# The first convolution layer of a graph network with its two products in the other order

## The chip, the cores and the metric

The kernel runs on one core of one Trainium2 chip. The core has five engines that run their own instruction streams and wait for each other by semaphores: TensorE (PE, matrix products into PSUM), VectorE (DVE), ScalarE (ACT), GpSimd (POOL) and SyncE (SP, which here only starts transfers). A transfer is carried out by 16 DMA engines. The metric is the device time of one execution in microseconds; the median of some executions is compared.

## The reference

`x` has 128 samples of 128 nodes with 128 features. A layer of graph convolution multiplies by weights, adds a bias, multiplies by the adjacency matrix over the nodes and cuts below zero. Two such layers, then four passes of an LSTM over windows of 1, 2, 3 and 4 nodes, a residual sum with a normalization, then a graph attention with another residual sum and normalization.

```
h = relu(einsum('ts,bsh->bth', adj, x @ Wg0 + bg0))
h = relu(einsum('ts,bsh->bth', adj, h @ Wg1 + bg1))
for p in range(1, 5):
    wins = h[:, :nw * p, :].reshape(Bv * nw, p, Hd)
    last = _lstm_last(Wih[p-1], Whh[p-1], bih[p-1], bhh[p-1], wins)
    h = h.at[:, idx, :].set(last.reshape(Bv, nw, Hd))
x = layernorm(x + h)
x = layernorm(x + attention(x, W_lin, W_val, a, W_out, adj, src, dst))
```

## The kernel before

Everything is computed to about single precision. Some products are plain FP32 products: a 128x128 by 128x128 product then appears as two records ("passes") in the trace. Others are made of three F32R products over 512 columns: each operand is split into a rounded part (`_hi`) and the rest (`_lo`), and hi*hi, lo*hi and hi*lo are added in PSUM.

**Stages.** The span has three parts. The first (to about 211 us) is the convolution stage, fused with the LSTM pass over windows of one node. The second is the LSTM passes over 2, 3 and 4 nodes (lines 429 to 474 on TensorE). The third is the attention (function `back`). This case is about the first.

**Slots.** The samples are cut into 32 tiles of four samples, 512 columns each. The first stage runs through 38 slots. It is a pipeline written out by hand: slot n works on tile n in the first product, tile n-1 in the second, and so on. Each engine has its own `slot(n)` function that gives its order of work, and runs it strictly in that order. On TensorE slot n does:

- L361: x times adjacency (bank AX), tile n, four FP32 products with the x tile of one sample stationary
- L351 to L353: the LSTM's input gate, tile n-5, three F32R products
- L379: times Wg0 (bank H1), tile n-1, four FP32 products
- L351 to L353: the candidate gate G, tile n-5
- L389: times adjacency (bank AH), tile n-2, four FP32 products
- L351 to L353: the output gate, tile n-5
- L402 to L406: bias and times Wg1 (bank H2), tile n-3, four F32R products

On ScalarE: L510 relu and rounding of bank H2 into hT_hi, L515 copy of bank AX into axT, L500 for gates I and G, L524 rounding of bank AH, L529 tanh of the cell, L500 for the output gate. On VectorE: L709 output (gate times tanh), L713 rest of H2 into hT_lo (semaphore h2_done), L719 and L721 split of the output, L730 relu of bank H1 into h1, L737 cell value (semaphore c_ready, which L529 waits for), L741 rest of bank AH.

**What else lies between slots.** After some slots TensorE turns a piece of LSTM weights (L285, four transposes), ScalarE rounds it (L492, w_hi) and VectorE takes the rest (L700, w_lo). `piece_slot` puts these after slots 2, 11, 14, 17, 20, 23 and 26. The text calls it a cut. After slots 0 to 6 come small preparations for the attention: `rank_rows` after slot 0 and `sort_edges` after slot 1 (L314, L317) on TensorE. On VectorE `degrees`, `rank_edges` and `rank_rows` (lines 578 to 630, up to L603) stand ahead of slot 0, since they only prepare tables; L586 in `degrees` sums the LSTM biases once they are loaded. L634 reads what sort_edges has made.

**Transfers.** SyncE loads x tiles into a ring of three (L232), each as soon as L361 has read the tile three before it. The tile has nodes on partitions, and the four samples' rows of 128 features are 512 bytes each. Wg0 is requested right behind the first tile. ScalarE's queue loads biases and Wg1 at the start. For the third stage a second array, x_by_feature, with features first, is loaded.

Of the kernel before, what the change touches and what calls it, by code (L numbers as in the profile page):

```python
# [7 lines left out]
F32 = mybir.dt.float32  # L8
F32R = mybir.dt.float32r
# [3 lines left out]
P = 128  # L13
# [9 lines left out]
BT = 4  # L23
# [62 lines left out]
        self.bias = sb("bias", [P, SKIPS * GATES])  # L86


def front(nc, sb, sem, tables, hT_hi, hT_lo, ident, adj_sb, psum, x, adj, Wg0, bg0, Wg1, bg1, Wih, Whh, bih, bhh,
          W_lin, W_val, a, W_out, src, dst):  # L90

    B = x.shape[0]
    tiles = B // BT
    phases = lstm_phases(B)
    TW = BT * P
    HEADS, DH = a.shape  # L100
# [19 lines left out]
    tanh_c = [work[:, 11 + s, :] for s in range(2)]  # L120
    h_full = [work[:, 13 + s, :] for s in range(2)]

    axT = [work[:, s, :] for s in range(2)]
    h1 = [work[:, 2 + s, :].rearrange("p (b h) -> p b h", b=BT) for s in range(2)]
    X_RING = 3
    x_tile = [work[:, k, :].rearrange("p (b d) -> p b d", b=BT) for k in (8, 10, 11)]
    w_raw = [work[:, k, :].rearrange("p (g d) -> p g d", g=GATES) for k in (5, 13)]

    adjT = sb("adjT", [P, P])
    wg0 = sb("wg0", [P, P])  # L130
    wg1 = sb("wg1", [P, P])
    wg1_hi = sb("wg1_hi", [P, P], F32R)
# [42 lines left out]
    names = ("ident_zero ident_ready consts zeros row_ones adj_loaded wg0_loaded wg1_loaded bg0_loaded bg1_loaded col_loaded b_loaded "  # L175
             "adjT_psum adjT_ready neg_bg0 degree_psum degree_ready by_ready ranks_psum deg_hi bias_hi deg_ready bias_ready "
             "b_summed b_psum b_ready wg1_cut wg1_ready w_psum w_hi_ready w_lo_ready "
             "ax_psum axT_ready h1_psum h1_ready ah_psum ahT_hi ahT_ready h2_psum h2_hi h2_done "
             "gates_read f_ready ig_ready tanh_ready fc_done ig_done c_ready h_mul h_hi h_done tiles_done "
             "rows_loaded cols_loaded a_loaded iota_done a_zero tables_f ecol_done key_done spreads ranks permutes rows_psum rows_ready "  # L180
             "row_edges onehots w_means w_centred wT_psum wT_ready adj_psum adj_done eps_done log_done diag_done log_psum log_ready ends_ready sames shifted caps")
# [3 lines left out]
    gate_psum = [sem(f"f_gate_psum_{n}") for n in "ifgo"]  # L185
    CREDIT = 2

    AX, H1, AH, H2 = range(4)
    GATE_BANK = {I: 4, G: 5, O: 6}
    SIDE = 7  # L190

# [4 lines left out]
    def has(k):  # L196
        return 0 <= k < tiles
# [31 lines left out]

    def run_sync(sp):  # L230
        def load_x(k):
            sp.dma_start(x_tile[k % X_RING], x[k * BT:(k + 1) * BT].rearrange("b t d -> t b d")).then_inc(x_loaded[k % X_RING], 16)  # L232

        def load_piece(i):
            p, j = pieces[i]
            s, _ = raw_of(i)
            sp.dma_start(w_raw[s], (Wih, Whh)[j][p].rearrange("(g h) d -> h g d", g=GATES)).then_inc(raw_loaded[s], 16)

        sp.dma_start(adj_sb[:, :], adj).then_inc(S["adj_loaded"], 16)
        load_x(0)  # L240
        sp.dma_start(wg0[:, :], Wg0).then_inc(S["wg0_loaded"], 16)
        sp.dma_start(edge_row_i[:, :], src.rearrange("(a e) -> a e", a=1).broadcast_to([P, E])).then_inc(S["rows_loaded"], 16)
        load_x(1)
        load_piece(0)
        for j, w in enumerate((W_lin, W_val, W_out)):
            sp.dma_start(w_raw[1][:, j, :], w).then_inc(raw_loaded[1], 16)
        load_x(2)
        for n in range(SLOTS):
            if has(n) and has(n + X_RING):
                sp.wait_ge(S["ax_psum"], n + 1)  # L250
                load_x(n + X_RING)
            if n == piece_slot[0]:
                sp.wait_ge(S["w_psum"], 1)
                load_piece(1)
                sp.wait_ge(S["wT_psum"], 1)
                load_piece(2)
            elif n in piece_slot and piece_slot.index(n) + 2 < len(pieces):
                i = piece_slot.index(n)
                sp.wait_ge(S["w_psum"], i + 1)
                load_piece(i + 2)  # L260
# [16 lines left out]
    def run_tensor(pe, entry):  # L277
# [77 lines left out]
        def slot(n):  # L355
            if has(n):
                pe.wait_ge(x_loaded[n % X_RING], 16 * (n // X_RING + 1))
                if n:
                    pe.wait_ge(S["axT_ready"], n)
                for b in range(BT):  # L360
                    mm = pe.matmul(psum[:, AX, b * P:(b + 1) * P], x_tile[n % X_RING][:, b, :], adjT[:, :], start=True, stop=True)  # L361
                mm.then_inc(S["ax_psum"], 1)
            if has(n - 5):
                if n == 5:
                    pe.wait_ge(S["w_lo_ready"], 1)
                    pe.wait_ge(S["b_ready"], 1)
                    pe.wait_ge(S["deg_ready"], 1)
                    pe.wait_ge(S["bias_ready"], 1)
                    pe.wait_ge(S["rows_ready"], 2)
                gate_product(I, n - 5)  # L370
            if has(n - 1):
                k = n - 1
                pe.wait_ge(S["axT_ready"], k + 1)
                if k:
                    pe.wait_ge(S["h1_ready"], k)
                else:
                    pe.wait_ge(S["wg0_loaded"], 16)
                for b in range(BT):
                    mm = pe.matmul(psum[:, H1, b * P:(b + 1) * P], axT[k % 2][:, b * P:(b + 1) * P], wg0[:, :], start=True, stop=True)  # L379
                mm.then_inc(S["h1_psum"], 1)  # L380
            if has(n - 5):
                gate_product(G, n - 5)
            if has(n - 2):
                k = n - 2
                pe.wait_ge(S["h1_ready"], k + 1)
                if k:
                    pe.wait_ge(S["ahT_ready"], k)
                for b in range(BT):
                    mm = pe.matmul(by_batch(psum[:, AH, :])[:, b, :], h1[k % 2][:, b, :], adjT[:, :], start=True, stop=True)  # L389
                mm.then_inc(S["ah_psum"], 1)  # L390
            if has(n - 5):
                gate_product(O, n - 5)
            if has(n - 3):
                k = n - 3
                if k:
                    pe.wait_ge(S["h2_done"], k)
                else:
                    pe.wait_ge(S["deg_ready"], 1)
                    pe.wait_ge(S["bias_ready"], 1)
                    pe.wait_ge(S["wg1_ready"], 1)  # L400
                out, cols = psum[:, H2, :], block_of(k)
                pe.matmul(out, bias_rows[:, :], deg_rows[:, :, :], start=True, stop=False)  # L402
                pe.wait_ge(S["ahT_ready"], k + 1)
                pe.matmul(out, wg1_hi[:, :], hT_hi[:, cols], start=False, stop=False)
                pe.matmul(out, wg1_hi[:, :], hT_lo[:, cols], start=False, stop=False)
                pe.matmul(out, wg1_lo[:, :], hT_hi[:, cols], start=False, stop=True).then_inc(S["h2_psum"], 1)  # L406
# [69 lines left out]
    def run_scalar(act, entry):  # L476
# [29 lines left out]
        def slot(n):  # L506
            if has(n - 4):
                k = n - 4
                act.wait_ge(S["h2_psum"], k + 1)
                act.activation(hT_hi[:, block_of(k)], psum[:, H2, :], ACT.Relu).then_inc(S["h2_hi"], 1)  # L510
            if has(n):
                act.wait_ge(S["ax_psum"], n + 1)
                if n >= 2:
                    act.wait_ge(S["h1_psum"], n - 1)
                act.activation(axT[n % 2], psum[:, AX, :], ACT.Copy).then_inc(S["axT_ready"], 1)  # L515
            if has(n - 5):
                if n == 5:
                    act.wait_ge(S["b_ready"], 1)
                gate_of(I, n - 5)
                gate_of(G, n - 5)  # L520
            if has(n - 2):
                k = n - 2
                act.wait_ge(S["ah_psum"], k + 1)
                act.activation(hT_hi[:, block_of(k)], psum[:, AH, :], ACT.Copy).then_inc(S["ahT_hi"], 1)  # L524
            if has(n - 5):
                k = n - 5
                act.wait_ge(S["c_ready"], k + 1)
                act.wait_ge(S["h_mul"], CREDIT + k)
                act.activation(tanh_c[1], cell[1], ACT.Tanh).then_inc(S["tanh_ready"], 1)  # L529
                gate_of(O, k)  # L530
# [46 lines left out]
    def run_vector(dve, entry):  # L577
# [125 lines left out]
        def slot(n):  # L703
# [12 lines left out]
            if has(n - 6):  # L716
# [3 lines left out]
                dve.wait_ge(S["h_hi"], k + 1)  # L720
                dve.tensor_tensor(hT_lo[:, block_of(k)], h_full[1], hT_hi[:, block_of(k)].bitcast(F32),  # L721
                                  ALU.subtract).then_inc(S["tiles_done"], 1)
            if has(n - 1):
                k = n - 1
                dve.wait_ge(S["h1_psum"], k + 1)
# [24 lines left out]
        dve.tensor_scalar(bg0_all[:, :], bg0_all[:, :], -1.0, None, ALU.mult).then_inc(S["neg_bg0"], 1)  # L750
        dve.wait_ge(S["adjT_psum"], 1)
        dve.tensor_copy(adjT[:, :], psum[:, SIDE, 0:P]).then_inc(S["adjT_ready"], 1)
        degrees()
        rank_edges()
        rank_rows()
# [660 lines left out]
    return Part(S, 0, None, run_sync, run_gpsimd, run_tensor, run_scalar, run_vector), entry  # L1416


def program(nc, x, xt, adj, Wg0, bg0, Wg1, bg1, Wih, Whh, bih, bhh, W_lin, W_val, a, W_out, src, dst, out):
    B = x.shape[0]  # L1420
    with ExitStack() as ctx:
        def held(name, shape, dt=F32):
            return ctx.enter_context(nc.sbuf_tensor(name, shape, dt))
# [10 lines left out]

        with ExitStack() as room:
            first = front(nc, lambda name, shape, dt=F32: room.enter_context(nc.sbuf_tensor(name, shape, dt)), sem, tables, hT_hi, hT_lo,
                          ident, adj_sb, psum, x, adj, Wg0, bg0, Wg1, bg1, Wih, Whh, bih, bhh, W_lin, W_val, a, W_out, src, dst)
        with ExitStack() as room:
            second, entry = back(nc, lambda name, shape, dt=F32: room.enter_context(nc.sbuf_tensor(name, shape, dt)), sem, tables, first,
                          hT_hi, hT_lo, ident, psum, xt, a, src, out)  # L1440
# [52 lines left out]
```

## Time and profile before

| | |
|---|---|
| median of 3 runs | 916.77 us |
| the three runs | 914.58, 916.77, 917.51 us |
| profiled execution, its own time | 916.78 us |
| its span | 915.0 us |
| busy TensorE, VectorE, ScalarE, GpSimd | 96%, 76%, 67%, 19% |
| convolution stage with the first LSTM pass | to about 211 us |

The span runs from the first to the last instruction of the profile; the rest of the execution's time lies around it. An engine counts as busy while it executes an instruction, also when several overlap in its pipeline. On TensorE a record's duration includes the drain of the array, so the next record starts before it ends, and what a product costs is the time from its start to the next start. "Idle before" names the time that an engine stood still ahead of an instruction and which instruction or transfer released it.

### The profile page before, as it was taken

What the parts mean: (1) busy time and instruction counts of PE and PEld (TensorE: products, weight loads), DVE (VectorE), ACT (ScalarE), POOL (GpSimd) and SP (SyncE); (2) the same over time, 40 slices, a digit from 0 to 9 for tenths busy, and PEclk for the clock granted to TensorE, in tenths of its full rate; (3) what the DMA queues carried; (4) which work ended last, traced back from release to release, by engine and by line L of the source; (5) the groups of instructions that cost most, each with busy time, mean ns of one, the idle gap of its engine ahead of it and who ended that gap; (6) DMA issues with size and microseconds to landing.
All of it is one profiled execution on the core that took longest, in us unless ns stands there. A gap on an engine that the chain in (4) does not pass through costs nothing.

```text
span 915.0 us, 15431 instructions
## 1 busy us (share of the span) xinstructions
PE 876.2 (96%) x5411; PEld 761.5 (83%) x5411; DVE 694.7 (76%) x1560; ACT 612.2 (67%) x1116; POOL 175.0 (19%) x509
## 2 busy tenths in 40 slices
PE   6999999999999999999999999999998999999795
PEld 6888888877787779999998887877787888887684
DVE  4777777777778787778777777676787887886885
ACT  1777777777777666676676666666786677775344
POOL 0000000000000000000000010012564455655665
PEclk9999999999999999999999999999999999999998
DMA  4211221001000000000000177775360011111122
GB/s 108 73 47 58 70 59 47 24 1 47 1 1 0 1 1 1 1 1 1 1 1 1 29 156 162 161 183 139 81 151 1 25 36 31 29 37 47 36 70 70
DMA packets 43260, 45.44 MB, mean 50 GB/s; under 512 B 2576, under 2 KB 40112, under 8 KB 40112
## 3 DMA queue, kind: packets, MB, share of 16 engines
q1 hardware_dynamic: 39504, 27.47, 10.5%
q0 software_dynamic: 2304, 16.78, 9.0%
q8 instruction: 44, 0.72, 0.3%
q10 hardware_dynamic: 1376, 0.22, 0.1%
q14 instruction: 32, 0.26, 0.1%
HBM read 19.29 MB, written 8.39 MB: 30 GB/s over the span
## 4 chain that ended last, share of the span: by engine, by line
PE 76%; DVE 8%; DMA 6%; issue 5%; ACT 2%; POOL 1%; ACTq 0%; DVEq 0%; POOLq 0%
PE psum L443 7%; PE psum L444 7%; PE psum L445 7%; PE psum L1135 6%; PE psum L1062 6%; PE psum L461 5%; PE psum L457 5%; PE psum L458 5%; DMA hT_lo<-x_stage 3%; PE psum L361 3%; PE psum L379 3%; PE psum L389 3%; PE psum L1146 2%; PE psum L1118 2%; PE psum L352 2%
## 5 line engine op out<-in xcount | busy, mean ns | idle before, releaser
L561 ACT ACTIVATE work<-psum,bias 128x512 f32<-128x512 f32 (+1 forms) x408 | 233.3, 623 | 29.2 <-PE psum L461 28.6
L443 PE MATMUL psum<-hT_hi,w_hi 128*128 128x512 f32 (+1 forms) x408 | 148.7, 365 | 3.3 <-ACT work L561 2.6
L444 PE MATMUL psum<-hT_lo,w_hi 128*128 128x512 f32 (+1 forms) x408 | 147.4, 361 | 0.0
L445 PE MATMUL psum<-hT_hi,w_lo 128*128 128x512 f32 (+1 forms) x408 | 147.2, 361 | 0.0
L545 ACT ACTIVATE work<-work 128x512 f32<-128x512 f32 (+1 forms) x112 | 63.8, 570 | 104.4 <-DVE work L813 73.1
L973 POOL DMA_DIRECT2D hT_lo<-hT_hi x8 | 7.3, 918 | 558.5 <-DVE hT_lo L788 539.3
L820 DVE TENSOR_TENSOR work<-work 128x512 f32<-128x512 f32 (+1 forms) x112 | 68.5, 612 | 54.1 <-ACT work L545 54.1
L457 PE MATMUL psum<-hs_hi,w_hi 128*128 128x512 f32 (+1 forms) x288 | 103.8, 360 | 0.8 <-DVE hs_hi L786 0.7
L461 PE MATMUL psum<-hs_lo,w_hi 128*128 128x512 f32 (+1 forms) x288 | 104.4, 362 | 0.0
L458 PE MATMUL psum<-hs_hi,w_lo 128*128 128x512 f32 (+1 forms) x288 | 103.1, 358 | 0.0
L443 PEld LDWEIGHTS psum<-hT_hi,w_hi 128*128 128x128 f32 x408 | 76.8, 188 | 17.5 <-ACT work L561 5.4
L445 PEld LDWEIGHTS psum<-hT_hi,w_lo 128*128 128x128 f32 x408 | 76.8, 188 | 10.8
L444 PEld LDWEIGHTS psum<-hT_lo,w_hi 128*128 128x128 f32 x408 | 76.8, 188 | 10.0
L500 ACT ACTIVATE work<-psum,bias 128x512 f32<-128x512 f32 x96 | 64.9, 682 | 27.0 <-PE psum L353 24.6
L806 DVE TENSOR_TENSOR work<-work 128x512 f32<-128x512 f32 (+1 forms) x112 | 68.2, 609 | 19.1 <-ACT work L561 19.1
L1135 PE MATMUL psum<-from_node,va 128*128 128x128 f32 x512 | 63.7, 278 | 5.0 <-DVE x_kept L1364 4.4
L1062 PE MATMUL psum<-w_qv,y_ordered 128*128 128x128 f32 x512 | 63.7, 277 | 3.4 <-DVE hT_lo L1305 3.4
L1135 PEld LDWEIGHTS psum<-from_node,va 128*128 128x128 f32 x512 | 59.7, 192 | 7.4 <-issue 4.8
L1062 PEld LDWEIGHTS psum<-w_qv,y_ordered 128*128 128x128 f32 x512 | 60.7, 193 | 3.8 <-issue 3.6
L461 PEld LDWEIGHTS psum<-hs_lo,w_hi 128*128 128x128 f32 x288 | 54.0, 188 | 10.2 <-DVE hs_lo L788 4.0
L457 PEld LDWEIGHTS psum<-hs_hi,w_hi 128*128 128x128 f32 x288 | 54.1, 188 | 9.5 <-DVE hs_hi L786 3.0
L1012 POOL TENSOR_TENSOR rstd<-var_eps,minus_half 128x4 f32<-128x4 f32 (+1 forms) x49 | 60.5, 1235 | 3.8
(191 smaller groups left out, 1856.4 us busy)
## 6 DMA issues: line engine op xcount, KB each, us to landing
work<-x SPq DMA_DIRECT2D x32, 256.0 KB, 3.0
x_stage<-x_by_feature SPq DMA_DIRECT2D x8, 1024.0 KB, 5.2
hT_lo<-hT_hi POOLq DMA_DIRECT2D x8, 1024.0 KB, 9.2
hT_lo<-x_stage POOLq DMA_DIRECT2D x8, 1024.0 KB, 7.0
out<-x_kept SPq DMA_DIRECT2D x32, 256.0 KB, 2.3
work<-L_gnn_Wih SPq DMA_DIRECT2D x4, 256.0 KB, 3.0
work<-L_gnn_Whh SPq DMA_DIRECT2D x3, 256.0 KB, 3.0
bg_all<-L_gnn_bg ACTq DMA_DIRECT2D x2, 64.0 KB, 5.6
```

Of the source, the lines that this page charges most:

```text
L443: pe.matmul(out, w_hi[:, w, g, :], xh, start=True, stop=False)
L444: pe.matmul(out, w_hi[:, w, g, :], xl, start=False, stop=False)
L445: mm = pe.matmul(out, w_lo[:, w, g, :], xh, start=False, stop=(t == 0))
L457: pe.matmul(out, w_hi[:, w, g, :], hh, start=False, stop=False)
L458: pe.matmul(out, w_lo[:, w, g, :], hh, start=False, stop=False)
L461: pe.matmul(out, w_hi[:, w, g, :], hl, start=False, stop=True).then_inc(gate_psum[g], 1)
L500: op = act.activation(gate[1][g], psum[:, GATE_BANK[g], :], ACT.Tanh if g == G else ACT.Sigmoid, bias=bias[:, g:g + 1])
L561: op = act.activation(gate[s][g][:, 0:ph.width], psum[:, 4 * s + g, 0:ph.width], ACT.Tanh if g == G else ACT.Sigmoid, bias=bias[:, b:b + 1])
L806: op = dve.tensor_tensor(i_g, gate[s][I][:, 0:ph.width], gate[s][G][:, 0:ph.width], ALU.mult)
L820: dve.tensor_tensor(h_full[s][:, 0:ph.width], gate[s][O][:, 0:ph.width], tanh_c[s][:, 0:ph.width], ALU.mult).then_inc(S["h_mul"], 1)
L1062: mm = pe.matmul(psum[:, bank, b * P:(b + 1) * P], y_ordered[:, k % 2, b, :], w, start=True, stop=True)
L1135: mm = pe.matmul(psum[:, sum_bank(k), b * P:(b + 1) * P], va[:, k % 2, c, b * P:(b + 1) * P], from_node[:, c, :], start=(c == 0), stop=(c ...
```

## The change

The first layer, relu(adj (x Wg0 + bg0)), is computed as adj times (x Wg0) in place of (adj x) times Wg0.

- The first product of slot n (bank now called XW) multiplies the x tile by Wg0, in four FP32 products as before. Since the x tile is the stationary operand and is contracted over features, it now has to lie with features on partitions: the host gives the array x_by_batch, 32 tiles of 128 features by 512 values, and a tile is one run of 2 KB on each partition.
- ScalarE's L515 writes the rounded part xw_hi (in buffers that the LSTM uses only later) in place of axT. VectorE gets a new operation, xw_lo = bank XW - xw_hi, between L721 and L730 of a slot. It signals xw_ready.
- The second product of slot n multiplies by the adjacency as three F32R products of 512 columns with adjT_hi and adjT_lo stationary, in place of four FP32 products.
- TensorE's first product of slot n waits for xw_ready of slot n-1 (bank XW is free only then), where it waited for ScalarE's axT_ready. In slot 0 it waits for Wg0.
- adjT is split once, behind L752.

```diff
-    axT = [work[:, s, :] for s in range(2)]
+    xw_hi, xw_lo = hs_hi, hs_lo
+    adjT_hi = sb("adjT_hi", [P, P], F32R)
+    adjT_lo = sb("adjT_lo", [P, P], F32R)
 def load_x(k):
-            sp.dma_start(x_tile[k % X_RING], x[k * BT:(k + 1) * BT].rearrange("b t d -> t b d")).then_inc(x_loaded[k % X_RING], 16)
+            sp.dma_start(x_tile[k % X_RING], xb[k]).then_inc(x_loaded[k % X_RING], 16)
 TensorE, slot
             if has(n):
                 pe.wait_ge(x_loaded[n % X_RING], 16 * (n // X_RING + 1))
                 if n:
-                    pe.wait_ge(S["axT_ready"], n)
+                    pe.wait_ge(S["xw_ready"], n)
+                else:
+                    pe.wait_ge(S["wg0_loaded"], 16)
                 for b in range(BT):
-                    mm = pe.matmul(psum[:, AX, b * P:(b + 1) * P], x_tile[n % X_RING][:, b, :], adjT[:, :], start=True, stop=True)
-                mm.then_inc(S["ax_psum"], 1)
+                    mm = pe.matmul(psum[:, XW, b * P:(b + 1) * P], x_tile[n % X_RING][:, b, :], wg0[:, :], start=True, stop=True)
+                mm.then_inc(S["xw_psum"], 1)
             if has(n - 1):
                 k = n - 1
-                pe.wait_ge(S["axT_ready"], k + 1)
                 if k:
                     pe.wait_ge(S["h1_ready"], k)
                 else:
-                    pe.wait_ge(S["wg0_loaded"], 16)
-                for b in range(BT):
-                    mm = pe.matmul(psum[:, H1, b * P:(b + 1) * P], axT[k % 2][:, b * P:(b + 1) * P], wg0[:, :], start=True, stop=True)
-                mm.then_inc(S["h1_psum"], 1)
+                    pe.wait_ge(S["adjT_split"], 1)
+                pe.wait_ge(S["xw_ready"], k + 1)
+                out = psum[:, H1, :]
+                pe.matmul(out, adjT_hi[:, :], xw_hi[:, k % 2], start=True, stop=False)
+                pe.matmul(out, adjT_lo[:, :], xw_hi[:, k % 2], start=False, stop=False)
+                pe.matmul(out, adjT_hi[:, :], xw_lo[:, k % 2], start=False, stop=True).then_inc(S["h1_psum"], 1)
 ScalarE, slot
-                act.wait_ge(S["ax_psum"], n + 1)
+                act.wait_ge(S["xw_psum"], n + 1)
                 if n >= 2:
                     act.wait_ge(S["h1_psum"], n - 1)
-                act.activation(axT[n % 2], psum[:, AX, :], ACT.Copy).then_inc(S["axT_ready"], 1)
+                act.activation(xw_hi[:, n % 2], psum[:, XW, :], ACT.Copy).then_inc(S["xw_hi"], 1)
 VectorE, slot, between L721 and L730
+            if has(n):
+                dve.wait_ge(S["xw_hi"], n + 1)
+                dve.tensor_tensor(xw_lo[:, n % 2], psum[:, XW, :], xw_hi[:, n % 2].bitcast(F32), ALU.subtract).then_inc(S["xw_ready"], 1)
 VectorE, behind L752
+        dve.wait_ge(S["adjT_ready"], 1)
+        dve.tensor_copy(adjT_hi[:, :], adjT[:, :]).then_inc(S["adjT_cut"], 1)
+        dve.wait_ge(S["adjT_cut"], 1)
+        dve.tensor_tensor(adjT_lo[:, :], adjT[:, :], adjT_hi[:, :].bitcast(F32), ALU.subtract).then_inc(S["adjT_split"], 1)
```

## Rows read from the trace of the kernel before

**Rows 1.** The page: busy time, share of the span, instructions of each engine.
```profile
PE 876.2 (96%) x5411; PEld 761.5 (83%) x5411; DVE 694.7 (76%) x1560; ACT 612.2 (67%) x1116; POOL 175.0 (19%) x509
```
**Rows 2.** Timeline of TensorE, slot 17: start us, us, engine, line, operation, [idle before].
```profile
103.64 1.06 PE L379 MATMUL psum<-wg,work 128*128 128x128 f32 x8
104.45 0.48 PE L351 MATMUL psum<-hT_hi,w_hi 128*128 128x512 f32 x1
...
105.24 1.06 PE L389 MATMUL psum<-adjT,work 128*128 128x128 f32 x8
```
**Rows 3.** Timeline of TensorE, slot 33, where no L361 and no L379 is left.
```profile
194.59 0.39 PE L351 MATMUL psum<-hT_hi,w_hi 128*128 128x512 f32 x1
...
195.29 0.40 PE L351 MATMUL psum<-hT_hi,w_hi 128*128 128x512 f32 x1
```
**Rows 4.** Timeline of VectorE, slot 31 and the first operation of slot 32.
```profile
184.45 0.69 DVE L709 TENSOR_TENSOR work<-work 128x512 f32<-128x512 f32 x1 [0.53 <-ACT work L500]
...
188.16 0.69 DVE L737 TENSOR_TENSOR work<-work 128x512 f32<-128x512 f32 x1 [0.73 <-ACT work L500]
...
190.18 0.69 DVE L709 TENSOR_TENSOR work<-work 128x512 f32<-128x512 f32 x1 [0.53 <-ACT work L500]
```
**Rows 5.** Timelines of VectorE and ScalarE, the rest of slot 32.
```profile
193.05 0.68 DVE L737 TENSOR_TENSOR work<-work 128x512 f32<-128x512 f32 x1
...
195.07 0.69 DVE L709 TENSOR_TENSOR work<-work 128x512 f32<-128x512 f32 x1 [0.59 <-ACT work L500]
...
194.31 0.67 ACT L500 ACTIVATE work<-psum,bias 128x512 f32<-128x512 f32 x1
194.88 0.59 ACT L510 ACTIVATE hT_hi<-psum 128x512 fp32r<-128x512 f32 x1
```
**Rows 6.** Timelines of TensorE, ScalarE, VectorE around the cut after slot 11.
```profile
72.51 0.60 PE L285 MATMUL psum<-ident,work 128*128 128x128 f32 x4
72.94 1.06 PE L361 MATMUL psum<-adjT,work 128*128 128x128 f32 x8
...
73.14 0.60 ACT L492 ACTIVATE w_hi<-psum 128x512 fp32r<-128x512 f32 x1 [0.32 <-PE psum L285]
...
73.77 0.69 DVE L700 TENSOR_TENSOR w_lo<-psum,w_hi 128x512 fp32r<-128x512 f32 x1 [1.38 <-ACT w_hi L492]
74.38 0.68 DVE L709 TENSOR_TENSOR work<-work 128x512 f32<-128x512 f32 x1
```
**Rows 7.** Timeline of VectorE, the start.
```profile
11.87 0.28 DVE L586 TENSOR_TENSOR b_sum<-b_raw 16x128 f32<-16x128 f32 x1 [2.94 <-DMA b_raw<-L_gnn_bhh]
...
17.98 0.69 DVE L730 TENSOR_TENSOR work<-psum,neg_bias 128x512 f32<-128x512 f32 x1
19.78 0.69 DVE L634 COPY permute<-psum 128x512 f32<-128x512 f32 x1 [1.10 <-PE psum L317]
...
23.19 0.69 DVE L741 TENSOR_TENSOR hT_lo<-psum,hT_hi 128x512 fp32r<-128x512 f32 x1 [0.62 <-ACT hT_hi L524]
```
**Rows 8.** Timeline of TensorE, the start, slots 0, 1, 4 and 5.
```profile
7.03 2.07 PE L361 MATMUL psum<-adjT,work 128*128 128x128 f32 x8 [1.33 <-DMA work<-x]
...
12.99 2.08 PE L361 MATMUL psum<-adjT,work 128*128 128x128 f32 x8
...
16.57 2.39 PE L314 MATMUL psum<-permute,spread 128*128 128x256 f32 x8
...
30.89 0.49 PE L402 MATMUL psum<-deg_rows,bias_rows 66*128 66x512 f32 x1 [0.54 <-DVE hT_lo L713]
...
31.93 1.06 PE L361 MATMUL psum<-adjT,work 128*128 128x128 f32 x8
```
**Rows 9.** Windows of the start: each engine's busy time, granted clock, DMA share, GB/s.
```profile
12.00:16.00 4.00, 4.00 (x19) 3.64 (x19) 3.89 (x19) 0.60 (x1) 0.00 (x0) 1.00 0.02 4
```
**Rows 10.** DMA queues, packets, MB, share: 0 to 12 us, then 212 to 224 us.
```profile
q1 hardware_dynamic: 3470, 1.75, 60.7%
...
q1 hardware_dynamic: 144, 1.05, 25.1%
```

More of the change, by code:

```diff
@@ L86, in __init__, with front @@
         self.bias = sb("bias", [P, SKIPS * GATES])
-def front(nc, sb, sem, tables, hT_hi, hT_lo, ident, adj_sb, psum, x, adj, Wg0, bg0, Wg1, bg1, Wih, Whh, bih, bhh,
+def front(nc, sb, sem, tables, hT_hi, hT_lo, ident, adj_sb, psum, xb, adj, Wg0, bg0, Wg1, bg1, Wih, Whh, bih, bhh,
           W_lin, W_val, a, W_out, src, dst):
-    B = x.shape[0]
-    tiles = B // BT
+    tiles = xb.shape[0]
+    B = tiles * BT
     phases = lstm_phases(B)
@@ L121, in front @@
     h_full = [work[:, 13 + s, :] for s in range(2)]
-    axT = [work[:, s, :] for s in range(2)]
+    xw_hi, xw_lo = hs_hi, hs_lo
     h1 = [work[:, 2 + s, :].rearrange("p (b h) -> p b h", b=BT) for s in range(2)]
     X_RING = 3
-    x_tile = [work[:, k, :].rearrange("p (b d) -> p b d", b=BT) for k in (8, 10, 11)]
+    x_tile = [work[:, k, :].rearrange("p (b t) -> p b t", b=BT) for k in (8, 10, 11)]
     w_raw = [work[:, k, :].rearrange("p (g d) -> p g d", g=GATES) for k in (5, 13)]
     adjT = sb("adjT", [P, P])
+    adjT_hi = sb("adjT_hi", [P, P], F32R)
+    adjT_lo = sb("adjT_lo", [P, P], F32R)
     wg0 = sb("wg0", [P, P])
@@ L177, in front @@
              "b_summed b_psum b_ready wg1_cut wg1_ready w_psum w_hi_ready w_lo_ready "
-             "ax_psum axT_ready h1_psum h1_ready ah_psum ahT_hi ahT_ready h2_psum h2_hi h2_done "
+             "xw_psum xw_hi xw_ready adjT_cut adjT_split h1_psum h1_ready ah_psum ahT_hi ahT_ready h2_psum h2_hi h2_done "
              "gates_read f_ready ig_ready tanh_ready fc_done ig_done c_ready h_mul h_hi h_done tiles_done "
@@ L186, in front @@
     CREDIT = 2
-    AX, H1, AH, H2 = range(4)
+    XW, H1, AH, H2 = range(4)
     GATE_BANK = {I: 4, G: 5, O: 6}
@@ L249, in run_sync @@
             if has(n) and has(n + X_RING):
-                sp.wait_ge(S["ax_psum"], n + 1)
+                sp.wait_ge(S["xw_psum"], n + 1)
                 load_x(n + X_RING)
@@ L1416, in back, with program @@
     return Part(S, 0, None, run_sync, run_gpsimd, run_tensor, run_scalar, run_vector), entry
-def program(nc, x, xt, adj, Wg0, bg0, Wg1, bg1, Wih, Whh, bih, bhh, W_lin, W_val, a, W_out, src, dst, out):
-    B = x.shape[0]
+def program(nc, xb, xt, adj, Wg0, bg0, Wg1, bg1, Wih, Whh, bih, bhh, W_lin, W_val, a, W_out, src, dst, out):
+    B = xb.shape[0] * BT
     with ExitStack() as ctx:
@@ L1436, in program @@
             first = front(nc, lambda name, shape, dt=F32: room.enter_context(nc.sbuf_tensor(name, shape, dt)), sem, tables, hT_hi, hT_lo,
-                          ident, adj_sb, psum, x, adj, Wg0, bg0, Wg1, bg1, Wih, Whh, bih, bhh, W_lin, W_val, a, W_out, src, dst)
+                          ident, adj_sb, psum, xb, adj, Wg0, bg0, Wg1, bg1, Wih, Whh, bih, bhh, W_lin, W_val, a, W_out, src, dst)
         with ExitStack() as room:
@@ L1478 @@
     nc = bacc.Bacc("TRN2", target_bir_lowering=False, num_devices=1, dynamic_dma_scratch_size=1024)
-    arrays, args = {}, []
-    for name in _INPUTS:
-        array = np.ascontiguousarray(inputs[name])
-        arrays[name] = array
-        args.append(nc.dram_tensor(name, array.shape, mybir.dt.from_np(array.dtype), kind="ExternalInput").ap())
-    B, N, D = arrays["x"].shape
-    group = lstm_phases(B)[-1].batches
-    by_feature = arrays["x"].reshape(B // group, group // BT, BT, N, D).transpose(0, 4, 1, 3, 2)
-    arrays["x_by_feature"] = np.ascontiguousarray(by_feature).reshape(B // group, D, group * N)
-    args.insert(1, nc.dram_tensor("x_by_feature", arrays["x_by_feature"].shape, F32, kind="ExternalInput").ap())
-    args.append(nc.dram_tensor("out", arrays["x"].shape, F32, kind="ExternalOutput").ap())
+    arrays = {name: np.ascontiguousarray(inputs[name]) for name in _INPUTS}
+    x = arrays.pop("x")
+    B, N, D = x.shape
+    group = lstm_phases(B)[-1].batches
+    by_state = x.reshape(B // group, group // BT, BT, N, D).transpose(0, 4, 1, 3, 2)
+    arrays = {"x_by_batch": np.ascontiguousarray(x.reshape(B // BT, BT, N, D).transpose(0, 3, 1, 2)),
+              "x_by_state": np.ascontiguousarray(by_state).reshape(B // group, D, group * N), **arrays}
+    args = [nc.dram_tensor(name, array.shape, mybir.dt.from_np(array.dtype), kind="ExternalInput").ap() for name, array in arrays.items()]
+    args.append(nc.dram_tensor("out", x.shape, F32, kind="ExternalOutput").ap())
     program(nc, *args)
```

## The prediction

> **What bounds the kernel now.** I read first the engines' shares: TensorE is busy 96% of the span, VectorE 76%, ScalarE 67% [rows 1]. That says who leads on average; what the change is worth is read from the stage that it touches, so the next view is TensorE in order of time in one slot of the convolution stage. There every FP32 block of four products (eight passes) holds TensorE 0.81 us, 103.64 to 104.45, and a group of three F32R products of 512 columns that follows an FP32 block holds it 0.79 us, 104.45 to 105.24, with no idle time between [rows 2]. Further on, where a group of three follows F32R products, it takes 0.70 us, 194.59 to 195.29: its first record is 0.39 us long and not 0.48 [rows 3]. So the change of kind costs 0.09 us besides the products. The third view is VectorE over the same slots: a slot lasts 190.18 - 184.45 = 5.73 us, and L737 starts after 0.73 us of idle time, released by ScalarE's gate, which had waited for TensorE [rows 4]. TensorE sets the pace, with VectorE close behind.
>
> How close is to be seen one slot later, where TensorE has no L361 block to do and is the faster one. There L737 starts straight behind L730, at 193.05, with no idle time, and the next L709 comes at 195.07, after tanh and output gate on ScalarE [rows 5]. From L709 to L709 this is 195.07 - 190.18 = 4.89 us [rows 4, 5]. This is a closed loop: VectorE runs L709, L713, L719, L721, L730, L737 in order, ScalarE's L529 needs L737, the output gate L500 follows L529, the next L709 needs that gate. It goes round in 4.89 us whatever TensorE does; up to slot 31 it has 5.73 - 4.89 = 0.84 us to spare.
>
> **The change part by part.**
>
> *The second product.* Removed in each slot is L379's FP32 block, added three F32R products with adjT_hi and adjT_lo stationary. Block and G group took 0.81 + 0.79; now both follow F32R products and take 0.70 each. Saving 1.60 - 1.40 = 0.20 us a slot, so a full slot would last 5.53. There are 28 slots that have both (5 to 32): 5.6 us, if TensorE stays the bound. The first product keeps form and count (x stationary, Wg0 moving) and costs the same. ScalarE's L515 writes xw_hi instead of axT, from the same bank in the same size: nothing.
>
> *The new subtraction on VectorE* (xw_lo). It has the form of L700, PSUM minus its rounded part over 512 columns, and L700 holds VectorE 74.38 - 73.77 = 0.61 us [rows 6]. It stands between L721 and L730, hence inside the loop: 4.89 + 0.61 = 5.50 us against TensorE's 5.53. In a plain slot it is hidden with 0.03 us left. Its cover is gone in the six slots after 8 in which weights are cut (11, 14, 17, 20, 23, 26). There ScalarE does w_hi (0.60) behind the output gate and VectorE L700 (0.61) ahead of L709 [rows 6]. ScalarE's next starts 194.88 - 194.31 = 0.57 after the gate where the loop's L709 started 195.07 - 194.31 = 0.76 after it [rows 5], so the loop grows by 0.57 + 0.60 + 0.03 + 0.61 - 0.76 = 1.05 us, and TensorE's slot only by the four transposes, 72.94 - 72.51 = 0.43 [rows 6]. Three slots with one cut cost the loop 16.50 + 1.05 = 17.55 and TensorE 16.59 + 0.43 = 17.02. Before, the loop had 2 x 0.84 to recover in; now it has 0.06. From the first cut on the loop leads, half a microsecond more each time. At first only VectorE lags; TensorE waits for xw_ready once the lag passes some 2 us, which I expect from slot 20 on. The lag is paid in full even where TensorE does not yet wait, since from slot 32 on the loop sets the end of the stage [rows 5].
>
> *The wait for xw_ready at the start.* So far L361 of slot 1 waited for ScalarE alone. Now it waits for VectorE's subtraction of slot 0, and ahead of that VectorE has rank_edges and rank_rows: it is busy without a gap from L586 at 11.87, when the last bias lands, to L730 at 17.98 [rows 7]. Queued behind the waiting L361 on TensorE are slot 1's H1 product and sort_edges, and L634 on VectorE waits for these. Step by step: subtraction 17.98 to 18.67; L361 of slot 1 from 18.72 instead of 12.99. At that stage its block takes 2.08 us against 1.06 later on, twice the time [rows 2, 8]; I take 1.87 to the next start (0.2 less, as in later blocks), then H1 at half pace 2 x 0.70 = 1.40, so L314 of sort_edges starts at 18.72 + 1.87 + 1.40 = 21.99 instead of 16.57 [rows 8], and L634, which came 3.21 us behind it at 19.78 [rows 7], at 25.20: 5.4 us later. From there to the H2 product at 30.89, released by L713 on VectorE [rows 8], VectorE is nearly always busy; two more subtractions (slots 2 and 3) make 1.22 us, of which the 0.62 idle before L741 at 23.19 [rows 7] takes up half. Slot 5's L361 comes 5.4 + 0.5 = 5.9 us later than 31.93 [rows 8].
>
> The granted clock reads 1.00 from 12 to 16 us [rows 9], the upper level, while the blocks take double time; how long TensorE stays at that pace after waiting 5.7 us is not to be seen. Bounds: at full pace throughout, L361 and H1 take 0.9 + 0.7 instead of 3.27, which with sort_edges a little faster is 2.0 us back; if it stays slow until slot 2 is done, about 1 us more. I take the middle, as the block at 12.99 was still slow 6 us after the one at 7.03, with little to do between them [rows 8]. The Trainium skill (TensorE: Matmul & The Clock Gate, section "The HAM clock gate") says that the idle state is the throttled one and activity releases it. That agrees with blocks at double time here and with my slow value; with the full-pace end the sum would be 918.7.
>
> *x laid out by feature.* A tile has 128 runs of 2 KB in place of 512 of 512 B, with the same bytes. In steady state the loads have slots to spare, so nothing. At the start they share the DMA engines with the bias that releases L586. By the queue's rows a small packet takes 0.607 x 16 x 12 us / 3470 = 34 ns, one of 7.3 KB takes 0.251 x 16 x 12 / 144 = 335 ns [rows 10], which is 94 ns for 2 KB against 134 for four small ones. On three early tiles (1536 packets, 3.2 us of all engines) that is up to 1.0 us earlier. Against it, the larger pieces may hold up the small loads of the other queue; I allow as much to the other side and take 0. The Trainium skill (DMA: Bandwidth & Descriptors, section "Specifications") puts the smallest transfer at line rate at 512 B; by it the gain is nothing, which the rate of the rows contradicts by up to 30%. With the rows' rate the sum would be 919.7.
>
> *The split of adjT.* Two 128x128 operations of VectorE, about 0.3 us each, stand behind L752 while it waits for DMAs and TensorE ahead of L586: nothing. Their first user, H1 of slot 0, comes at 20.6. Wg0, now needed in slot 0, is requested right behind the first x tile; a few tenths there move only L361 of slot 0, whose result nobody needs before 17.98.
>
> **The sum.** L709 of slot 12, just behind the first cut, is at 74.38 [rows 6]. It moves by +5.9 and by 7 x -0.20 for slots 5 to 11: 78.88. Then 20 turns of the loop at 5.50 and five cuts at 1.05 make 115.25: L709 of slot 32 at 194.13 instead of 190.18 [rows 4], that is +3.95. Behind it nothing changes, since from slot 32 on neither xw operation is left, and the later phases begin later by that much. The profiled execution took 916.78 (span 915.0), as good as the median of 916.77: 920.7 us.
>
> **The rivals.**
> *TensorE stays the bound.* If the loop turns a few hundredths faster than its rows add up to, or the cut's work overlaps better, all 5.6 us come through and cancel the start: +0.3, 917.1 us. This ends on the other side: no measurable change. It decides at a loop of 5.32 us, where three turns and a cut fit into TensorE's 17.02. For it: the room in a plain slot, 0.03 us, is no more than the rounding of the rows, and VectorE is not full. Against: the turn of 4.89 is measured without any wait for TensorE.
> *The start costs less.* Full pace of TensorE, or the bias 1 us earlier and a shorter chain: -2 to -3 from the forecast, 918.2.
> *The start costs more or both VectorE and ScalarE lose.* TensorE slow until 26, small loads held up, or a loop of 5.56: +1.5 to +2, 922.5.
> *Faster than before.* Only TensorE as bound together with a cheap start: 0.3 - 2.0 - 1.0 = -2.7, 914.1.
>
> **How the numbers follow.** Forecast 0.50, TensorE the bound 0.20, cheaper start 0.14, dearer 0.12, faster 0.04. A measurement of this kernel can tell about 0.3%, 2.75 us, so slower begins at 919.5. The forecast has most of its weight above that (0.45 of 0.50), the dearer start all: with a little of the cheaper one 0.60 slower. Same 0.37, faster 0.03. The likeliest case spans 919 to 922; the range takes in TensorE as bound below and the dearer start above: 916.2 to 922.8.
>
> **What would show it.** In the profile after: L361 of slot 1 on TensorE near 18.7, released by VectorE's subtraction; slot 5's L361 near 37.8; L737 on VectorE with next to no idle time in front from slot 12 on; TensorE idle before L361 from about slot 20, for some 0.5 us at each cut; the G group 0.70 after the H1 product. Wrong would be: an idle time of several tenths before L737 to the end of the stage, L361 of slot 1 before 17, or a subtraction much longer than 0.61.

## The result and the profile after

| | before | changed |
|---|---|---|
| median | 916.15 us (914.58 to 917.51, 5 runs) | 919.96 us (919.22 to 921.34, 5 runs) |
| ratio | | 1.0047, 95% interval 1.0035 to 1.0059 |
| profiled execution, its own time | 916.78 us | 919.47 us |
| its span | 915.0 us | 917.7 us |

The changed kernel is slower by 3.8 us, clear of noise. The forecast was 920.7 us, 3.9 more than the execution it was summed on. That the two numbers are so close is partly luck, as the parts below show.

The page of the changed kernel, engines' busy time; it answers rows 1:

```profile
PE 870.9 (95%) x5251; PEld 749.5 (82%) x5251; DVE 710.4 (77%) x1594; ACT 605.0 (66%) x1116; POOL 174.6 (19%) x509
```

TensorE has 160 matmul records fewer and VectorE 34 instructions more. The lines of the code have moved: the first product L361 is now L366, the second L384 to L386, the output L709 is L715, the relu of bank H1 L739, the cell value L746; the new subtraction is L731.

Timeline of TensorE after, the start; it answers rows 8 (columns as there):

```profile
17.48 2.04 PE L366 MATMUL psum<-wg,work 128*128 128x128 f32 x8 [6.08 <-DVE hs_lo L731]
19.18 0.77 PE L384 MATMUL psum<-hs_hi,adjT_hi 128*128 128x512 f32 x1
...
20.60 2.34 PE L317 MATMUL psum<-permute,spread 128*128 128x256 f32 x8
...
36.09 1.05 PE L366 MATMUL psum<-wg,work 128*128 128x128 f32 x8
...
37.68 0.40 PE L384 MATMUL psum<-hs_hi,adjT_hi 128*128 128x512 f32 x1
...
38.37 0.40 PE L354 MATMUL psum<-hT_hi,w_hi 128*128 128x512 f32 x1
...
39.06 1.05 PE L395 MATMUL psum<-adjT,work 128*128 128x128 f32 x8
```

TensorE stands still for 6.08 us ahead of slot 1, released by the new subtraction. The first two products and the first part of sort_edges (L317 here) then run with long records, 2.04 us instead of 1.05 for the first product, as slot 1's did before. Slot 5's first product starts at 36.09 instead of 31.93. Its second product takes 38.37 - 37.68 = 0.69 us and the G group behind it 39.06 - 38.37 = 0.69 (predicted 0.70 each).

Timeline of VectorE after: the start, then slots 12 to 15; it answers rows 7, 4 and 6.

```profile
10.53 0.28 DVE L592 TENSOR_TENSOR b_sum<-b_raw 16x128 f32<-16x128 f32 x1 [2.65 <-DMA b_raw<-L_gnn_bhh]
...
16.64 0.69 DVE L731 TENSOR_TENSOR hs_lo<-psum,hs_hi 128x512 fp32r<-128x512 f32 x1
...
23.76 0.69 DVE L640 COPY permute<-psum 128x512 f32<-128x512 f32 x1 [2.23 <-PE psum L320]
...
76.34 0.69 DVE L706 TENSOR_TENSOR w_lo<-psum,w_hi 128x512 fp32r<-128x512 f32 x1 [1.38 <-ACT w_hi L498]
76.95 0.68 DVE L715 TENSOR_TENSOR work<-work 128x512 f32<-128x512 f32 x1
...
82.42 0.69 DVE L715 TENSOR_TENSOR work<-work 128x512 f32<-128x512 f32 x1 [0.73 <-ACT work L535]
...
84.69 0.68 DVE L731 TENSOR_TENSOR hs_lo<-psum,hs_hi 128x512 fp32r<-128x512 f32 x1
85.29 0.68 DVE L739 TENSOR_TENSOR work<-psum,neg_bias 128x512 f32<-128x512 f32 x1
85.89 0.68 DVE L746 TENSOR_TENSOR work<-work 128x512 f32<-128x512 f32 x1
...
87.90 0.69 DVE L715 TENSOR_TENSOR work<-work 128x512 f32<-128x512 f32 x1 [0.73 <-ACT work L535]
...
94.42 0.68 DVE L715 TENSOR_TENSOR work<-work 128x512 f32<-128x512 f32 x1
```

Before, the cell value of slot 31 waited 0.73 us for ScalarE's gate, and with it for TensorE [rows 4]. Now L746 starts 0.60 us behind L739, with no idle time. A turn of the loop is 87.90 - 82.42 = 5.48 us, the next, with a cut in it, 94.42 - 87.90 = 6.52. So it goes on to slot 32. L731 is the new subtraction, L739 the relu. The waits of TensorE in that stretch, 75 to 191 us, are in total (waiting line, what it waited for, us, times, longest):

```profile
PE psum L366 <- DVE hs_lo L731: 0.9, 3, 0.3
```

The view shows three short waits, at 132.48, 149.95 and 167.44, behind the cuts after slots 20, 23 and 26. TensorE's timeline shows that each costs more than its idle time. The first two rows are the last product of slot 21 and the first of slot 22, the others the same place one slot later, where nothing is waited for:

```profile
131.78 0.39 PE L412 MATMUL psum<-hT_hi,wg_lo 128*128 128x512 f32 x1
132.48 1.13 PE L366 MATMUL psum<-wg,work 128*128 128x128 f32 x8 [0.31 <-DVE hs_lo L731]
...
137.82 0.39 PE L412 MATMUL psum<-hT_hi,wg_lo 128*128 128x512 f32 x1
138.05 1.05 PE L366 MATMUL psum<-wg,work 128*128 128x128 f32 x8
```

From start to start it is 0.70 us with the wait and 0.23 without, so the wait costs 0.47 us. Idle time is counted only from the end of the record before, and 0.31 is left of it. With the wait, slots 21 to 23 of TensorE last 5.97 + 5.57 + 5.94 = 17.48 us, exactly three turns of the loop (5.48 + 5.48 + 6.52); slots 12 to 14, where TensorE still leads itself, last 16.95. That is the trap of this profile: TensorE looks busy in nearly the whole stretch, and yet it is not what decides when the stage ends. The output operation of slot 32 is at 191.75 instead of 190.18 and the stage's last one at 213.31 instead of 211.73.

### The profile page after: what moved, and what is told of

The parts are those of the page before. It is cut to its first block, busy times and chain, and to the rows that moved or that the text cites. A ratio compares the mean times of both kernels' runs of the same rounds, so it can differ in the third digit from the quotient of the medians.

```text
span 917.7 us, 15146 instructions
## 1 busy us (share of the span) xinstructions
PE 870.9 (95%) x5251; PEld 749.5 (82%) x5251; DVE 710.4 (77%) x1594; ACT 605.0 (66%) x1116; POOL 174.6 (19%) x509
## 4 chain that ended last, share of the span: by engine, by line
PE 62%; DVE 7%; issue 4%; DMA 2%; ACT 2%; POOL 1%; ACTq 0%; DVEq 0%; POOLq 0%
PE psum L449 8%; PE psum L450 7%; PE psum L451 7%; PE psum L1148 6%; PE psum L467 6%; PE psum L1075 6%; PE psum L463 5%; PE psum L464 5%; PE psum L1159 2%; PE psum L1131 2%; PE psum L1102 2%; PE psum L1067 2%; DMA hT_lo<-x_stage 2%; PE psum L1092 1%; PE psum L1132 1%
```

## The experiments

Times in the sections below are compared with the kernel before on the same chip. "From slot 12 to 32" is the time from the output operation (L709 before, L715 changed) of slot 12 to that of slot 32, read from VectorE's timeline; it is 115.80 us before and 114.80 changed.

**The changed kernel again.** No edit.

> The changed kernel once more, as the base for its neighbours on one chip. Against the kernel before: 1.003 to 1.006. Landmarks as seen: slot 5's first product near 36.1 us, turn of the loop 5.48 us, L715 of slot 32 near 191.8 us.

Measured 919.89 us, ratio 1.0035 (1.0023 to 1.0048). Slot 5's first product 35.76, slot 12 to 32 114.81, end of the stage 212.96.

**The wait at the start.** Slot 0's subtraction goes ahead of the tables.

```diff
         degrees()
+        xw_rest(0)
         rank_edges()
         rank_rows()
...
-            if has(n):
+            if 0 < n < tiles:
                 xw_rest(n)      # the wait for xw_hi and the subtraction
```

> Slot 0's subtraction on VectorE is moved ahead of rank_edges and rank_rows; all else as changed. Theory (the start's loss is the wait for xw_ready behind the tables): slot 1's first product starts near 12.8 us instead of 17.5, sort_edges and L640 follow, slot 5's first product comes near 32.5 us instead of 36.1, and the rest keeps its pace: 3.4 us less than the changed kernel, so 1.000 to 1.001 of the kernel before. Rival (the start's loss comes from the two more subtractions in slots 2 and 3, or from TensorE at half pace): at most 1 us less.

Measured 914.29 us, ratio 0.9980 (0.9971 to 0.9989): 5.6 us less than the changed kernel, and 2.1 less than before. Its TensorE timeline:

```profile
12.11 2.08 PE L366 MATMUL psum<-wg,work 128*128 128x128 f32 x8
...
18.75 1.14 PE L366 MATMUL psum<-wg,work 128*128 128x128 f32 x8
...
31.26 1.05 PE L366 MATMUL psum<-wg,work 128*128 128x128 f32 x8
```

Slot 5 starts 4.5 us earlier than in the changed kernel on that chip, where 3.4 were expected, and the stage ends 4.5 us earlier (208.46). From slot 12 to 32 it takes 114.79 us, so nothing there has moved. The larger part of the start's loss is that one wait. It is not all: slot 5 still starts 1.5 us later than with the layout alone (29.77, below), of which 0.4 are a bias that landed later in this execution (10.99 against 10.59). The span of this execution is 5.0 us shorter; the other half microsecond lies behind the stage, where executions differ by as much.

**The place in the loop.** The subtraction goes behind the cell value.

```diff
                 dve.tensor_tensor(cell[1], gate[1][I], gate[1][G], ALU.mult).then_inc(S["c_ready"], 1)
+            if has(n):
+                xw_rest(n)
             if has(n - 2):
```

> The subtraction stands behind L746 (cell value) in each slot, so outside the loop of gate, L715 and L746, where VectorE waits for ScalarE; the start is as changed. Theory (the loop sets the pace from slot 12 on): the turn needs 4.9 us again, TensorE leads to slot 31 with slots of 5.53 us, and L715 of slot 32 comes near 188.9 instead of 191.8 us: 2.9 us less than the changed kernel. First product of the slot behind a cut waits some 0.1 us for xw_ready. Rival (TensorE stayed the bound, and the loss was the start alone): no change, within 0.5 us.

Measured 919.49 us, ratio 1.0031 (1.0020 to 1.0043): only 0.4 us less, and in the profiled execution the stage ends 0.6 us later (213.59 against 212.96). By the total the rival had won. The timelines say otherwise: slot 12 to 32 takes 112.96 us instead of 114.81, and VectorE waits again for the gate ahead of the cell value, as it did before the change. Two sound rows first, then the two that cost the gain, VectorE and then TensorE:

```profile
87.33 0.69 DVE L747 TENSOR_TENSOR work<-work 128x512 f32<-128x512 f32 x1 [0.43 <-ACT work L506]
87.94 0.69 DVE L711 TENSOR_TENSOR hs_lo<-psum,hs_hi 128x512 fp32r<-128x512 f32 x1
...
33.78 1.13 PE L366 MATMUL psum<-wg,work 128*128 128x128 f32 x8 [1.20 <-DVE hs_lo L711]
...
43.67 1.13 PE L366 MATMUL psum<-wg,work 128*128 128x128 f32 x8 [0.30 <-DVE hs_lo L711]
```

Slot 4's first product waits 1.20 us for slot 3's subtraction (0.72 in the changed kernel's first profile), which now stands behind the relu. Slot 6's waits for slot 5's subtraction, which also stands behind a cell value that comes late. Slot 5 starts at 37.63 us instead of 35.76, and slot 5 itself lasts 6.04 us instead of 5.50. Of the 1.9 us at slot 5, 0.7 are not the move's: the bias landed at 10.97 instead of 10.28, and slot 1's first product already started at 17.92 instead of 17.23. My 2.9 us had two errors. The place is bad for the first slots, by 1.2 and 0.5 us. And even with that mended (below) it is 153.8 us from slot 5's first product to slot 32's output, where my count of TensorE's slots had 152.8 and the changed kernel takes 155.7. This 1.0 us lies behind the cuts and is read below.

**Both moves.**

> Both moves: slot 0's subtraction ahead of the tables, the others behind L746. Theory: the two gains add, 6.3 us less than the changed kernel, 2.5 us less than the kernel before (0.997). Rival (they share one cause): no more than the better of the two alone.

Measured 913.27 us, ratio 0.9971 (0.9960 to 0.9983): 6.6 us less than the changed kernel. Slot 5 at 31.29, slot 12 to 32 112.94. The total is near the 6.3 expected, but not for the reason given: 5.6 us are the first move's and 1.0 is the second's, where 3.4 and 2.9 had been expected.

**The moves, each where it pays.** Slot 0 early, slots 1 to 5 between L727 and L739, from slot 6 on behind the cell value.

```diff
+            if 0 < n < 6:
+                xw_rest(n)
             if has(n - 1):
                 k = n - 1
                 dve.wait_ge(S["h1_psum"], k + 1)
...
                 dve.tensor_tensor(cell[1], gate[1][I], gate[1][G], ALU.mult).then_inc(S["c_ready"], 1)
+            if 6 <= n < tiles:
+                xw_rest(n)
```

> Slot 0's subtraction ahead of the tables, in slots 1 to 5 between L727 and L739 as in the changed kernel, from slot 6 on behind the cell value. Theory (the place behind the cell value cost its gain in the first slots, where the cell value or the work after it comes late): slot 5's first product near 31.3 us, slot 6's near 36.8 instead of 37.3, from L715's place in slot 12 to slot 32 112.95 us, end of the stage near 206.6 instead of 207.2 and 208.5; 0.5 us less than with both moves whole, 0.9965 of the kernel before. Rival (slots 1 to 5 don't matter): the same as with both moves whole.

Measured 912.47 us, ratio 0.9953 (0.9941 to 0.9966), the lowest of all, though its interval overlaps that of both moves whole. Slot 5 at 31.06 and slot 6 at 36.56, so 5.50 us apart; slot 12 to 32 112.97; end of the stage 206.41 (207.22 with both moves whole). These marks came as foretold, so what the place costs in the first slots is accounted for. The other 1.0 us is to be seen behind a cut, on VectorE and then on TensorE:

```profile
92.60 0.69 DVE L711 TENSOR_TENSOR hs_lo<-psum,hs_hi 128x512 fp32r<-128x512 f32 x1
...
92.97 0.39 PE L412 MATMUL psum<-hT_hi,wg_lo 128*128 128x512 f32 x1
93.43 1.13 PE L366 MATMUL psum<-wg,work 128*128 128x128 f32 x8
94.31 0.48 PE L354 MATMUL psum<-hT_hi,w_hi 128*128 128x512 f32 x1
```

The first product starts 0.83 us after the start of the subtraction, as at 132.48 in the changed kernel, and 0.46 us after L412 instead of 0.23. Its block then takes 0.88 us instead of 0.81. So the slots behind a cut last 5.73 and 5.58 us instead of 5.50, 0.3 us for each of six cuts, where 0.1 was expected. The row shows no idle time for it. Slots of 5.50 instead of 5.53 give 0.8 of these 1.8 us back.

**One more subtraction in the kernel before.** Its result is not used.

```diff
                 dve.wait_ge(S["h1_psum"], k + 1)
+                for j in range(1 if 6 <= n < tiles else 0):
+                    dve.tensor_tensor(hs_lo[:, (j + n * 1) % 2], psum[:, H1, :], hT_hi[:, block_of(n - 6)].bitcast(F32), ALU.subtract)
```

> The kernel before with one further subtraction of 512 columns on VectorE between L721 and L730 in slots 6 to 31, result unused. Theory (loop against TensorE): the turn needs 5.49 us and TensorE's slot 5.73; three slots with a cut need 17.5 in the loop and 17.6 on TensorE: hidden, under 0.3 us in all. Rival (work on VectorE costs its own length): 26 x 0.61, 15.9 us more.

Measured 915.86 us, ratio 0.9997 (0.9988 to 1.0006). Slot 12 to 32 takes 115.78 us, as without it. 26 operations of 0.61 us on the second busiest engine are free.

**Two more.** The same with `range(2 ...)` and `n * 2`, so two such subtractions in each of the slots 6 to 31.

> The kernel before with two further such subtractions in the same slots. Theory: the turn needs 6.09 us, over TensorE's 5.73, so 26 x 0.37 = 9.5 us and for six cuts 6 x (1.04 - 0.43) = 3.7 us: 13 us more, and TensorE idles. Rival (VectorE's busy share decides, which would rise to about 97% of a slot and still fit): under 2 us more.

Measured 929.34 us against 916.16, ratio 1.0140 (1.0125 to 1.0155): 13.2 us more than the kernel before, and 13.5 more than with one: so much for the same 26 operations once again. VectorE's timeline:

```profile
100.73 0.69 DVE L709 TENSOR_TENSOR work<-work 128x512 f32<-128x512 f32 x1 [0.73 <-ACT work L529]
...
106.81 0.69 DVE L709 TENSOR_TENSOR work<-work 128x512 f32<-128x512 f32 x1 [0.73 <-ACT work L529]
...
113.32 0.69 DVE L700 TENSOR_TENSOR w_lo<-psum,w_hi 128x512 fp32r<-128x512 f32 x1 [1.16 <-ACT w_hi L492]
113.92 0.68 DVE L709 TENSOR_TENSOR work<-work 128x512 f32<-128x512 f32 x1
```

The turn is 6.08 us and 7.11 with a cut: 4.89 and 2 x 0.60, and 1.03 for the cut. VectorE is idle for 0.73 us in each turn and the loop is full all the same, since in that time it waits for ScalarE's work on its own result. A count of busy time would have let the second operation in.

**The layout alone.** The kernel before, with x tiles by node in runs of 2 KB.

```diff
-            sp.dma_start(x_tile[k % X_RING], x[k * BT:(k + 1) * BT].rearrange("b t d -> t b d")).then_inc(x_loaded[k % X_RING], 16)
+            sp.dma_start(x_tile[k % X_RING], x[k]).then_inc(x_loaded[k % X_RING], 16)
```

> The kernel before with x handed over by node in tiles, so that a load is 128 runs of 2 KB in place of 512 of 512 B; products and order as before. Theory (fewer packets let the biases land earlier): L586 starts near 10.6 us instead of 11.9; TensorE's rank_rows waits for another load, so sort_edges and the slots gain 0.4 to 1.3 us; 0.9986 to 0.9996. Rival (the earlier bias in the changed kernel came from something else): L586 near 11.9, no change.

Measured 915.59 us, ratio 0.9997 (0.9986 to 1.0009). Timeline of TensorE:

```profile
9.68 0.66 PE L301 MATMUL psum<-adjT,by_degree 128*66 128x128 f32 x2 [2.05 <-DMA bg_all<-L_gnn_bg]
...
11.34 2.08 PE L361 MATMUL psum<-adjT,work 128*128 128x128 f32 x8
```

L586 starts at 10.59, 1.3 us earlier than in the profile before, L301 at 9.68 instead of 11.33, slot 5 at 29.77 instead of 31.93, and the stage ends at 209.57 instead of 211.73. The start of the old layout varies, though: the two kernels with idle subtractions, unchanged up to slot 5, start slot 5 at 30.85 and 31.44. So the layout brings 1 to 2 us there. In the total 0.6 is left, and the interval takes in nothing and 1.3. In this execution the last copy of the third part was issued 468.2 us behind the end of the stage, where the kernel before had it at 465.0; whether that belongs to the layout or to the execution was not settled. The total was expected at 0.9986 to 0.9996; at 0.9997 it can't be told from no change.

**The order alone.** New order and new layout, with the second product as one FP32 product and without a subtraction.

```diff
-                pe.matmul(out, adjT_hi[:, :], xw_hi[:, k % 2], start=True, stop=False)
-                pe.matmul(out, adjT_lo[:, :], xw_hi[:, k % 2], start=False, stop=False)
-                pe.matmul(out, adjT_hi[:, :], xw_lo[:, k % 2], start=False, stop=True).then_inc(S["h1_psum"], 1)
+                pe.matmul(out, adjT[:, :], xw[k % 2], start=True, stop=True).then_inc(S["h1_psum"], 1)
```

> The two products in the new order with the new layout, but the second as one FP32 product of 512 columns with adjT stationary: ScalarE copies bank XW, no subtraction, no wait of TensorE for VectorE. Theory (what the change gains and loses lies in the F32R form, its saving on TensorE and its subtraction on VectorE): it runs like the kernel before with the new layout: slot 5's first product near 29.8 us, a slot of 5.7 us, L715's place in slot 32 near 188.0, 0.999 of the kernel before. Rival (order or stationary operand matter by themselves): the second product's block differs from 0.81 us by more than 0.1, which moves the stage by over 3 us.

Measured 913.13 us, ratio 0.9959 (0.9946 to 0.9973). It beats the kernel before by more than was expected, and the changed kernel as well (0.9959 against 1.0035 and 1.0047). TensorE's timeline:

```profile
106.84 1.02 PE L384 MATMUL psum<-work,adjT 128*128 128x512 f32 x2
107.30 0.79 PE L354 MATMUL psum<-hT_hi,w_hi 128*128 128x512 f32 x1
107.94 0.40 PE L355 MATMUL psum<-hT_lo,w_hi 128*128 128x512 f32 x1
...
108.40 1.05 PE L393 MATMUL psum<-adjT,work 128*128 128x128 f32 x8
```

The second product and the G group hold TensorE from 106.84 to 108.40, 1.56 us: 0.04 less than in the form before and 0.18 more than in the changed one. How these split between the two can't be read, as the G group's first record starts under the tail of the product. A slot is 5.68 us. From the stage's end the gain is 3.6 us (208.10 against 211.73), of which 2.3 are there at slot 5 (29.60). The span is 5.4 us shorter than before, so 1.8 lies behind the stage. The time of this execution is only 3.9 us shorter (912.87 against 916.78): it is 3.3 us longer than its span, where the other kernels' profiled executions are 1.8 longer. Where that time lies stays open.

## Why the prediction was right, and where it was not

**The second product's saving** was 0.20 us a slot: 1.60 predicted down to 1.40, measured 0.69 + 0.69 = 1.38. Right in size; a slot led by TensorE lasts 5.50 to 5.51.

**The loop takes over** from the first cut on. Predicted turn 5.50, measured 5.48; a cut 1.05, measured 1.04; 20 turns and five cuts 115.25, measured 114.80. That it is the loop and not VectorE's work as such is shown by the pair of idle subtractions: one costs nothing, two cost 13.2 us, where 13 were foretold. What it costs the changed kernel is shown by the moves: behind the cell value the stretch takes 112.96, so the loop holds back 1.84 us of what TensorE saves. By my rows it was 115.25 - (20 x 5.53 + 5 x 0.43) = 2.5. The difference is that the stretch behind the cell value holds waits of its own, 0.3 us at each cut.

**TensorE's wait for the lag** came as forecast: some 0.5 us at each cut from about slot 20 on, measured 0.47 from start to start behind each of the cuts after slots 20, 23 and 26. The waits view alone, with 0.3 each, would have made it look overdone.

**The wait at the start** was the right mechanism at the wrong size. The step that failed is "5.9 us later" for slot 5: it was 4.2 (36.09 against 31.93), and 4.7 and 5.2 against the two kernels with idle subtractions, which are unchanged up to there. Inside it, half pace (1.87 + 1.40, measured 1.70 + 1.42 to the start of sort_edges) held. The term mis-sized is the layout's. I took 0 between -1.0 and +1.0; the bias landed at 10.53 instead of 11.87, which is 1.3 us, more than the bound from packet rates [rows 10]. All kernels with 2 KB runs have it at 10.28 to 10.99, all with 512 B at 11.68 to 11.87. The rule of the Trainium skill (DMA: Bandwidth & Descriptors, section "Specifications"), by which 512 B is enough for line rate, would have given nothing; with the layout alone the bias came 1.3 us earlier all the same. That is not a test of the rate itself, since 0.4 of the 1.3 us is an earlier issue of that load. The rest is small: L634 (now L640) moved by 3.98 and slot 5 by 4.16, so the subtractions of slots 2 and 3, less what the new form saves in these slots, cost 0.2 and not 0.5.

**The sum** said +3.95 us at slot 32. It was +1.57 in this execution: of the 2.38 us between, 1.74 lie in the start, 0.19 in slots 5 to 11, which gained 1.59 and not 1.4, and 0.45 in the loop's shorter turns. So the stage explains 1.6 of the 2.7 us between the two profiled spans.

**Behind the stage** I had nothing change. But 1.1 us more came there, and this is the part that made the total agree. It can be narrowed down: 386.0 us behind the end of the stage a copy hT_hi to hT_lo is issued, in all executions within 0.1 us. The next issue of GpSimd, which waits for it, follows 7.3 us later before and 9.5 in the changed kernel. Before, then changed, the waits of GpSimd's timeline:

```profile
597.68 0.87 POOL L973 DMA_DIRECT2D hT_lo<-hT_hi  x1 [9.81 <-DVE hT_lo L788]
604.99 1.03 POOL L979 DMA_DIRECT2D hT_lo<-x_stage  x1 [6.44 <-DMA hT_lo<-hT_hi]
```

```profile
599.31 0.87 POOL L986 DMA_DIRECT2D hT_lo<-hT_hi  x1 [10.36 <-DVE hT_lo L801]
608.85 0.86 POOL L992 DMA_DIRECT2D hT_lo<-x_stage  x1 [8.67 <-DMA hT_lo<-hT_hi]
```

All six profiles with the second product as F32R show 9.5, the five others 7.3 to 8.1. In the changed kernel two transfers of the kind "instruction" fall into this time, in the kernel before none. The queues' rows (packets, MB, share), changed kernel, 599.31 to 608.91 us:

```profile
q8 instruction: 1, 0.02, 0.6%
q14 instruction: 1, 0.01, 0.2%
```

The kernel with the order alone has one of the two there (q8), the one with two more subtractions the other (q14), and neither has the delay. That such transfers hold up the copy's end is only a guess; it was not tried. From there to the end the difference shrinks. From the end of the stage to the end of the span it is 703.6 to 704.4 us in the six profiles with the delay and 701.5 to 705.5 in the five without, so the delay does not by itself make the rest longer: the kernel with the layout alone has none and the longest rest (705.5). Which part of the 3.5 to 3.8 us of the medians is from there stays open: the stage holds 1.2 to 2.7 by the profiles (its end at 212.96 and 213.31, against 210.61 with one idle subtraction and 211.73 before), the rest is behind it or in the spread.

**The rivals.** TensorE as the bound would have left 112.8 from slot 12 to 32; the turn without idle time rules it out. A dearer start did not come. A cheaper start did, in part.

## What to carry to other kernels

Look for the loop that goes through several engines in program order, and time it where the bounding engine has nothing to do, as in the last slots here. In this kernel an operation in the loop was free as long as the loop was shorter than the bound's slot, whatever the busy share said, and was paid in full beyond that, even where the bounding engine showed no idle time. An operation that signals another engine is best placed where its own engine would wait anyway, but then look at the slots where that wait is missing: here the first slots and those behind a cut paid for the move. Its first instance has to stand ahead of the preparation, not behind. And a short wait costs more than its idle time says where records overlap: read it from start to start.

## What had not been expected of the hardware

- Loads of 256 KB in runs of 2 KB instead of 512 B let a small load in another queue land 1.3 us earlier at the start (10.59 against 11.87), with the same bytes. The small load's issue started at 4.25 us instead of 4.68, and from there it took 6.3 us to land instead of 7.2. In the first 12 us the hardware queue of the loads has 1968 packets instead of 3470, for 1.77 MB against 1.75.
- An FP32 product of 512 columns followed by an F32R group (1.56 us) costs 0.04 us less than four FP32 products of 128 columns with their own weights and the same group (1.60).
- VectorE's idle time in a plain turn was 1.26 us before (0.53 + 0.73), 0.73 with one idle subtraction, and still 0.73 with two, when the turn grew from 5.48 to 6.08 us: idle time of an engine in a loop need not be room.
- Behind a short wait of TensorE the FP32 block of four products took 0.88 us from start to start instead of 0.81.
